# A two-layer graph kernel: left scores routed through memory, weights loaded beside the first rows of x, a third adjacency buffer, degrees taken in layer 1, and the last pair finished tile by tile

## The reference, cut to what matters

```python
deg = jnp.maximum((adj != 0).astype(jnp.float32).sum(-1), 1.0)
h = jnp.maximum(_layernorm(x), 0.0)                  # x: 3327 x 256, adj: 3327 x 3327 of 0 and 1
# layer 0, with adj as both adjacencies
attn_a = sigmoid(concat([adj @ h, h]) @ Wa.T + ba)   # one number per row; attn_b the same with Wb
hs = h @ W_sa
s_left, s_right = hs @ a_sa[0, :256], hs @ a_sa[0, 256:]
e = where(adj != 0, exp(-leaky_relu(s_left[:, None] + s_right[None, :], 0.01)), 0)
x_a = (e / (sum(e, axis=1) + 1e-5)) @ hs
x_b = adj @ (h @ W_gcnb) + b_gcnb
x = x + sigmoid(attn_a * x_a + attn_b * x_b)
# layer 1
h = jnp.maximum(_layernorm(x), 0.0)
pooled = (adj + I) / deg @ h + h                     # deg**-0.5 on both sides, per row
x = x + relu(pooled @ W + b)
```

## Time and profile before

| | |
|---|---|
| median of 3 runs | 653.65 us (652.34 to 656.84) |
| the profiled execution's own time | 648.95 us |
| its span, first to last instruction | 647.1 us |
| PE busy | 617.8 us, 95% of the span |
| PE on the chain that ended last | 87% of the span |
| DVE / ACT / POOL busy | 438.2 / 365.3 / 271.5 us |
| mean granted PE clock | 0.986 of full speed |

### The profile page before, as it was taken

The page is one execution under the profiler, slowest core; times in us unless marked ns, Lnnn a source line. Parts: engine busy times, 40 slices in busy tenths (PEclk is TensorE's granted clock), DMA queues, the critical chain, the costliest instruction groups (busy, mean ns, idle before and its releaser), DMA issues.

```text
span 647.1 us, 13487 instructions
## 1 busy us (share of the span) xinstructions
PE 617.8 (95%) x5333; PEld 528.0 (82%) x5333; DVE 438.2 (68%) x869; ACT 365.3 (56%) x877; POOL 271.5 (42%) x378
## 2 busy tenths in 40 slices
PE   6777999999999999999999999999999799999994
PEld 3445677888888888888888888888888688888883
DVE  4577665799999898989898988988752323122131
ACT  2566676779888787878787777879632000000000
POOL 3547463355435162435353366313134253425331
PEclk9798999999999999999999999999999999999998
DMA  8904572397364554656563644000010365555521
GB/s 201 194 4 131 81 170 44 50 195 180 51 164 89 124 142 74 156 80 160 73 164 53 164 50 58 2 1 2 1 51 2 115 244 172 171 161 178 183 76 32
DMA packets 38549, 68.62 MB, mean 106 GB/s; under 512 B 3159, under 2 KB 30809, under 8 KB 37079
## 3 DMA queue, kind: packets, MB, share of 16 engines
q0 software_dynamic: 28544, 22.15, 23.6%
q1 hardware_dynamic: 7906, 41.68, 19.8%
q10 hardware_dynamic: 2037, 3.94, 2.3%
HBM read 67.74 MB, written 22.15 MB: 139 GB/s over the span
## 4 chain that ended last, share of the span: by engine, by line
PE 87%; POOL 4%; DVE 3%; issue 2%; DMA 1%; ACT 1%; ACTq 0%; POOLq 0%; DVEq 0%
PE accE L703 11%; PE accE L705 11%; PE accA L682 11%; PE accE L704 11%; PE accA L683 11%; PE accA L755 8%; PE accA L754 8%; PE accE L754 4%; PE accE L755 4%; POOL diag L337 1%; PE tp L610 1%; POOL stage L317 1%; PE pw L726 1%; PE pw L727 1%; PE pw L728 1%
## 5 line engine op out<-in xcount | busy, mean ns | idle before, releaser
L703 PE MATMUL accE<-HI,Z 128*128 128x257 f16 x676 | 184.3, 273 | 0.0
L705 PE MATMUL accE<-HI,E 128*128 128x257 f16 x676 | 184.1, 272 | 0.0
L704 PE MATMUL accE<-LO,Z 128*128 128x256 f16 x676 | 183.9, 272 | 0.0
L485 ACT ACTIVATE Z<-LO,sr 128x256 f32<-128x256 f32 x338 | 151.3, 497 | 40.0 <-PE accE L705 40.0
L682 PE MATMUL accA<-HI,adjT 128*128 128x258 f16 x676 | 154.1, 273 | 0.0
L683 PE MATMUL accA<-LO,adjT 128*128 128x258 f16 x676 | 154.0, 273 | 0.0
L494 ACT ACTIVATE Z<-Z,sr 128x256 f32<-128x256 f32 x338 | 150.2, 497 | 0.1
L945 DVE TENSOR_TENSOR E<-Z 128x512 bf16<-128x512 f32 x169 | 140.7, 832 | 5.8
L939 DVE TENSOR_TENSOR Z<-adjT,Z 128x512 f32<-128x512 bf16 x169 | 120.3, 712 | 18.8 <-ACT Z L494 18.6
L755 PE MATMUL accA<-LO,adjT 128*128 128x256 f16 x468 | 103.5, 273 | 0.0
L754 PE MATMUL accA<-HI,adjT 128*128 128x257 f16 x468 | 103.5, 273 | 0.0
(11 more groups left out here) (116 smaller groups left out, 761.6 us busy)
## 6 DMA issues: line engine op xcount, KB each, us to landing
adjT_store<-adjT SPq DMA_DIRECT2D x11, 1664.0 KB, 6.7
adjT<-adjT_store SPq DMA_DIRECT2D x11, 896.0 KB, 4.7
stage<-in_adj_dram POOLq DMA_DIRECT2D x48, 192.0 KB, 5.0
adjT<-adjT_store SPq DMA_DIRECT2D x11, 768.0 KB, 6.3
stage<-in_adj_dram POOLq DMA_DIRECT2D x36, 224.0 KB, 8.1
out_dram<-late ACTq DMA_DIRECT2D x12, 256.0 KB
stage<-in_adj_dram POOLq DMA_DIRECT2D x12, 223.5 KB, 9.7
xs<-in_x_dram SPq DMA_DIRECT2D x5, 256.0 KB, 6.0
```

Source lines behind the costliest of these rows:

```text
L485: ins = act.activation(Z[:, n % RING, v], slw[:, m], ACT.Relu, bias=sr99[:, t:t + 1], scale=1.0 - SLOPE)
L703: pe.matmul(dst[:, 0:D + 1], zhi, HI[:, t, 0:D + 1], start=(t == 0), stop=False)
L704: pe.matmul(dst[:, 0:D], zhi, LO[:, t, 0:D], start=False, stop=False)
L705: ins = pe.matmul(dst[:, 0:D + 1], zlo, HI[:, t, 0:D + 1], start=False, stop=(t == TILES - 1))
```

## The change

Five edits go together.

1. **Left scores through memory.** `diag`, `widen` and `left` go. SP stores the left-score column of a pair to a DRAM tensor `sl_store` (256 elements of 4 bytes), waits for it to land, and reads it back to `slw` with the same 1 KB row for all 128 partitions. `leaky(m, 0)` waits for that.
2. **Start.** The first x rows and the weights share the SP and ACT queues; DVE takes the first row statistics before the weight maxima; `dense(0)` comes ahead of `turn(1)` and `project(0)` on PE; throwaway matmuls are placed anew (44 in place of 50).
3. **Third buffer.** In layer 2 the raw adjacency buffer `stage` serves as a third buffer (`adj1`), used by `k` = 2, 5, 8, 11. The fillers around the last dense steps now take `pooled(2, ...)`.
4. **Degrees from layer 1.** The HI matmul of `neighbours` is 260 columns wide, with the ones column at its head; ACT copies the degree (`degs`); one DVE step inverts them all. `HI1` loses its ones column, and `output` is two fused operations per tile plus one.
5. **Last pair by tile.** For `k` = 12 all matmuls of tile 0 come first, then those of tile 1; output and store follow for each tile.

The diff, cut to its core:

```diff
+        adj1 = [adjT[1][:], adjT[0][:],
+                stage[:].rearrange("p e b q -> p (e b q)").rearrange("p (u e i v) -> p u e i v", u=PAIRS, e=2, v=2)]
...
         def _(sp):
-            for k, w in enumerate((W_sa, W_g)):
-                sp.dma_start(wsg[k], w.rearrange("(h p) o -> p h o", p=P)).then_inc(wsg_in, 16)
-            load_x(sp, 0, (2, 3))
+            load_x(sp, 0, (0, 1))
+            sp.dma_start(wsg[0], W_sa.rearrange("(h p) o -> p h o", p=P)).then_inc(wsg_in, 16)
...
+            def spread_left(i):
+                sp.wait_ge(srw_ok, i + 1)
+                sp.dma_start(bass.AP(sl_store.tensor, 2 * P * i, [[1, P], [P, 2]]), srw[:, 2 * i:2 * i + 2, 3],
+                             allow_slow_non_contiguous=True).then_inc(sl_out, 16)
+                sp.wait_ge(sl_out, 16 * (i + 1))
+                if i >= 1:
+                    sp.wait_ge(sl_in, 16 * i)
+                sp.dma_start(slw[:, i], bass.AP(sl_store.tensor, 2 * P * i, [[0, P], [1, 2 * P]])).then_inc(sl_in, 16)
...
+            for i in range(PAIRS):
+                spread_left(i)
+                if i == 0:
+                    sp.dma_start(w1, W1.rearrange("(h p) o -> p h o", p=P)).then_inc(w1_in, 16)
...
+                if i == 6:
+                    keep_adj(0)
+            for m in range(1, LAST - 1):
+                keep_adj(m)
...
+            sp.wait_ge(tr_ok, NC * PAIRS)
             for k in range(2, PAIRS):
                 for c, (u0, u1) in enumerate(CHUNKS):
-                    sp.wait_ge(part_done[c], k - 1)
-                    dst = adjT[(k + 1) % 2][:, u0:u1].rearrange("p u e i v -> p (u e i v)").bitcast(U32)
+                    if k >= 3:
+                        sp.wait_ge(part_done[c], k - 2)
+                    dst = adj1[k % 3][:, u0:u1].rearrange("p u e i v -> p (u e i v)").bitcast(U32)
...
             def score_parts(i):
...
-                if i >= 1:
-                    pool.wait_ge(wide, i)
-                for e in range(2):
-                    ins = pool.tensor_scalar(diag[:, e], ident[:], srw[:, 2 * i + e, 3:4], None, ALU.mult)
-                ins.then_inc(diag_ok, 1)
...
-            def widen(i):
-                pe.wait_ge(diag_ok, i + 1)
-                pe.matmul(pw[:, 256:512], ones[:], diag[:].rearrange("p e n -> p (e n)"), start=True,
-                          stop=True).then_inc(wide, 1)
...
-                        dst = bank(accA[m % 2], e)[:, 0:D + 2]
-                        pe.matmul(dst, w, HI[:, t, G0:HIW], start=(t == 0), stop=False)
-                        ins = pe.matmul(dst, w, LO[:, t, D:LOW], start=False, stop=(t == TILES - 1))
+                        dst = bank(accA[m % 2], e)
+                        pe.matmul(dst[:, 0:D + 4], w, HI[:, t, ONE:HIW], start=(t == 0), stop=False)
+                        ins = pe.matmul(dst[:, 2:D + 4], w, LO[:, t, D:LOW], start=False, stop=(t == TILES - 1))
...
             for s in range(PAIRS):
                 dense(s)
-                if s < 2:
-                    keep_busy(4)
-                widen(s)
+                if s == 0:
+                    turn(1)
+                    project(0)
...
-            row_stats(0)
-            scales(0, 3, 1)
-            minus_mean(0)
-            row_stats(1)
-            score_weights()
-            minus_mean(1)
+            row_stats(0)
+            gate_weights()
+            dve.wait_ge(wsg_in, 32)
+            largest(0, 2)
+            minus_mean(0)
+            largest(2, 3)
+            on_diagonal(0, 3)
+            row_stats(1)
+            scales(0, 3, 1)
+            turned_second(0)
...
+            for k in range(3, LAST):
                 for u in range(PAIRS):
                     pooled(k, u)
+            for e in range(2):
+                pooled_tile(LAST, e)
```

More of the change, by code:

```diff
@@ L90, in gnn_kernel @@
         wrows = sb("wrows", [8, P])
-        diag = sb("diag", [P, 2, P])
         ones = sb("ones", [P, P])
@@ L218, in gnn_kernel @@
         hi1_ok = sem("hi1_ok")
-        one1_ok = sem("one1_ok")
         lo1_ok = sem("lo1_ok")
-        adj_ld = [[sem(f"adj_ld{c}_{b}") for b in range(2)] for c in range(NC)]
+        adj_ld = [[sem(f"adj_ld{c}_{b}") for b in range(3)] for c in range(NC)]
         part_done = [sem(f"part_done{c}") for c in range(NC)]
@@ L260, in out_count @@
         def out_count(k, b):
-            return 16 * sum(3 if ORDER[j] == LAST else 1 for j in range(k + 1) if j % 2 == b)
+            return 16 * sum({LAST: 3, LAST - 2: 2}.get(ORDER[j], 1) for j in range(k + 1) if j % 2 == b)
         block = ctx.enter_context(nc.Block())
@@ L276, in _, with keep_adj @@
             load_x(sp, 3)
[L277 to L281, removed]
+            def spread_left(i):
[6 more added lines that the diff above has]
+                sp.dma_start(slw[:, i], bass.AP(sl_store.tensor, 2 * P * i, [[0, P], [1, 2 * P]])).then_inc(sl_in, 16)
+            def keep_adj(m):
                 sp.wait_ge(tr_ok, NC * (m + 1))
@@ L469, in first_halves @@
                     act.activation(dst, src[:, e], ACT.Copy).then_inc(hi_ok, 1)
-            def left(i):
-                act.wait_ge(wide, i + 1)
-                act.activation(slw[:, i], pw[:, 256:512], ACT.Copy).then_inc(sl_ok, 1)
             def leaky(m, u):
                 n = m * PAIRS + u
-                if n == 0:
-                    act.wait_ge(sl_ok, 1)
+                if u == 0:
+                    act.wait_ge(sl_in, 16 * (m + 1))
                 if m == 0:
@@ L538, in _ @@
             first_weights(1)
+            norm(1)
             for s in range(PAIRS + 5):
@@ L587, in store_out @@
                 m = ORDER[k]
+                if k == LAST:
+                    for e in range(2):
+                        act.wait_ge(o_ok, k + 1 + e)
+                        dst = bass.AP(out.tensor, (m * 64 + e) * D, [[QN * D, 4], [2 * D, QUAD], [1, D]])
+                        act.dma_start(dst, osb[k % 2][:, e]).then_inc(o_out[k % 2], 16)
+                    return
                 act.wait_ge(o_ok, k + 1)
@@ L1116, in output, with output_tile @@
                     dve.wait_ge(o_out[k % 2], out_count(k - 2, k % 2))
-                dve.scalar_tensor_tensor(out=osb[k % 2], in0=wx[:], scalar=0.0, in1=xs[:, 2 * m:2 * m + 2],
+                dve.scalar_tensor_tensor(out=osb[k % 2], in0=[wx, wm][k % 2][:], scalar=0.0, in1=xs[:, 2 * m:2 * m + 2],
                                          op0=ALU.max, op1=ALU.add).then_inc(o_ok, 1)
-            for k in range(PAIRS):
+            def output_tile(k, e):
+                dve.wait_ge(tile_done, e + 1)
+                dve.wait_ge(hpw_ok, k + 1)
+                dve.wait_ge(o_ok, k - 1)
+                pooled_out(k, e)
+                dve.wait_ge(y_ok, 2 * k + 1 + e)
+                dve.wait_ge(o_out[k % 2], out_count(k - 2, k % 2))
+                dve.scalar_tensor_tensor(out=osb[k % 2][:, e], in0=[wx, wm][k % 2][:, e], scalar=0.0,
+                                         in1=xs[:, 2 * ORDER[k] + e],
+                                         op0=ALU.max, op1=ALU.add).then_inc(o_ok, 1)
+            degrees()
+            for k in range(LAST):
                 output(k)
+            for e in range(2):
+                output_tile(LAST, e)
 _INS = ['x', 'adj', 'L0_gnn_W_sa', 'L0_gnn_a_sa', 'L0_gnn_W_gcnb', 'L0_gnn_b_gcnb', 'L0_gnn_Wa', 'L0_gnn_ba',
```

159 lines of the change are left out of this document (88 added, 71 removed).

## The result

| | before | after |
|---|---|---|
| median of four runs each | 655.25 us | 687.91 us |
| ratio, 95% interval | | 1.0505 [1.0447, 1.0563] |
| span of the profiled execution | 647.1 us | 682.7 us |

The change made the kernel 5% slower; 634.8 us (629 to 642) had been forecast. The two traces differ by 35.6 us, and they split it cleanly. The first transposes of layer 2's dense part started at 158.83 before and at 204.40 now: +45.6 us. From there to the same work of pair 11: 330.9 before, 331.2 now. From there to the first DVE operation behind the last matmul: 148.35 and 142.4, -6.0. From there to the end: 9.0 and 4.7, -4.3. So everything is lost ahead of these transposes, and the gains behind them are there.

What follows compares the result with a forecast made beforehand. PE was taken as busy throughout the long stretches, with gains left in the opening, float32 wide products, a layer 2 hole and the tail. -11 + 0.6 - 0.3 - 5.3 - 2.8 = -18.8 from 653.65 gave 634.8 us, range 629 to 642.

Steps and rivals of the forecast that it cites:

- T: Time of one left-score round trip through memory in SP's queue; 6.5 us would land the second adjacency store at 122.6, in time.
- third rival: SP's queue too slow: second adjacency store waits behind thirteen serial round trips; slower from T = 9.5, 667 us at 10.5; chance 0.06.
- the cover: Opening: new left-score transfers stay hidden, leaving at 20.5 and back by 32, before ACT needs them near 38.6 us; no cost.
- Start: Opening on PE: dense(0) starts at 16.2 us, 3.1 us earlier than before.
- Opening, pair by pair: Up to 60 us: dense products come earlier; -11 us, of which 5.6 is removed matmul time; bounds -13.5 and -6.
- the chain: Opening: each engine's order with old trace durations; dense products gain 3.9 us at the first, 10.2 at the sixth.
- Wider matmuls: Layer 1 neighbour matmuls: 676 HI matmuls grow from 258 to 260 columns, +0.6 us; bounds 0 and +2.
- Third buffer: Layer 2: wait for k = 2's second chunk and half clock after it go, -5.3 us; HI matmuls one column narrower, -0.3.
- Tail: Behind the last matmul: fewer DVE operations, -1.85 us, and a smaller last store, -1.0; -2.8 us in all.
- Rivals one and two: One: DVE holds the opening, which gives 6 us, 639.8, chance 0.19. Two: new wait in layer 2, 640.1, chance 0.08.

Runs made afterwards that it cites:

- (4): Kernel before plus scratch stores of a constant in layer 1, alone in SP's queue; 256 side-by-side 4-byte elements took 12.7, 10.7, 9.1 us issue to issue.
- (8): Kernel with 512-byte score rows, plus 12 throwaway matmuls before pair 1's dense product: 627.89 us; instead third buffer undone: 635.89; instead last pair as a pair: 633.41.
- (7): Changed kernel with each pair's score columns turned into two rows on PE, stored as 2 elements of 512 bytes: 629.06 us, ratio to before 0.9632.
- (2): Changed kernel with the float32 wide product back (diag, widen, left; nothing through memory), other four parts kept: 643.96 us, ratio to before 0.9824.
- 6: Changed kernel with left scores stored as 8-byte elements: 627.83 and 637.58 us; with second adjacency store also moved behind the ninth round trip: 625.73 us.

## Why the prediction was wrong

**The step that failed** is T = 6.5 us in the third rival, the time of a round trip, and in it the landing of the score column, for which the cover had put 5.9 us. Because of it the sum put the new transfers at nothing. Measured: the store landed in 11.8 us in the median of thirteen (7.5 to 14.5), T was 11.9, and the second adjacency store went out at 174.53. The other part of the cover, that the first row is back by 32, was late too (its read-back went out at 31.88 and took 4.7 us), but ACT reached its first score step only at 41.40, so this cost nothing.

The rival had the right place: the second adjacency store behind all round trips. Its form was right only in part, and that its figure agrees with the total is partly luck. By its line PE stands 13 T - 104 us for that store; with the measured 11.9 this is 51, and PE stood 52.3 for DVE in all, but 38.1 for the second store. The store landed at 183.0 and not at 192.8, since the first adjacency store, for which the line adds 8.8, took hardly a turn of its own in the series, and DVE came to the transpose that needs it at 141.8 and not at 125.5. It came late there because it had already waited 4.9 us for an adjacency load and 10.5 us for the first adjacency store, which the prediction did not price; PE's hole of 10.0 us stands behind the second of these.

The landing came from the nearest row of the same element size, the bias load of 5.9 us. That row reads 4-byte elements from memory; the new transfer writes them, side by side, and that took 9.1 to 12.7 us with nothing else in SP's queue (4). The argument against the rival, that the transfer engines are busy only 0.28 of the time, was empty: about half of the landing passed behind the store's last packet (5.5 of 11.8 us in the median), where idle engines are no help. Given that 6.5 left the store in time "by little", and that each microsecond of T costs 13, 0.06 was far too low a chance. The rule below 512 bytes that I cited from the Trainium skill ("DMA: Bandwidth & Descriptors", Specifications) warned of a slow store, and I set it aside with a row that did not measure the same thing. For the landing its limit is not what the runs show: 128 elements of 64 bytes took 4.7 and 4.8 us, 128 of 512 bytes 4.8 and 4.9. No run measured the rate, of which it speaks.

**Start:** forecast `dense(0)` at 16.2; it came at 15.82. Right.

**Opening, pair by pair:** forecast 24.4, 29.3, 34.9, 39.1, 46.1, 53.9; measured 23.9, 30.7, 36.0, 41.9, 48.6, 55.7. The gain at `dense(6)` was 8.4 us where the chain said 10.2; half clock came back at pairs 1 and 3 (granted clock 0.50 from 24 to 27 us and 0.51 from 36 to 39). Taking one such stretch away brought the next dense product 2.1 us forward (8), about as much as the difference. With a store that lands in time (7) the first transposes of layer 2 came at 150.29, 8.5 us earlier than before; with 8-byte elements and the moved store at 145.75, 13.1 earlier. The forecast of 11 lies between: right in size, once the transfers are hidden. The gain needs the wide product to go: with it in place the one trace shows none (2).

**Wider matmuls:** forecast +0.6; a pair took 30.36 us instead of 30.33, +0.3 over eleven pairs. Right in kind, half the size.

**Third buffer:** forecast -5.3 and -0.3; measured -6.0, and +6.8 when undone. Right.

**Tail:** forecast -2.8; measured -4.3. The mechanism was right. DVE's part was (2.8 to 0.94 us, -1.9); the last store's was forecast too small: the 6.2 us from DVE's end to the end of the span became 3.8, -2.4 instead of -1.0.

**Rivals one and two:** neither came. DVE did not hold the opening at 6 us, and no wait stood in layer 2.

So the sum of -18.8 fits what the change would have been without the landing, as far as the kernels of 6 and 7 tell, which differ from it in more than that: they ended at 625.7 and 629.1, by the traces 23.1 and 18.5 us below before, by the medians 28.1 and 23.6.

## What to carry to other kernels

A transfer that is off the path still has a place in its queue: multiply the time of a round trip by the number that stands ahead of the next thing somebody waits for, and compare with the moment when it is wanted; if little is left, measure the one transfer before trusting the sum. Take a landing from a row with the same direction, element size and neighbourhood, not only the same size. To spread a column through memory, bring it into rows or at least into elements of 8 bytes first.

## What the runs showed of the hardware that was not expected

- A store of 64 or more 4-byte elements side by side in device memory lands 5.1 to 8.9 us behind its last packet, in the stretches shown with the transfer engines idle: 6.6 to 12.7 us from issue to the next issue. The same 256 elements 64 or 512 bytes apart land 0.5 us behind it, 16 side by side 0.4 to 0.7, 128 elements of 8 bytes side by side 1.9 to 2.8, rows of 512 bytes 0.4 to 0.5.
- In the kernel these stores also delay other loads. From 60 to 110 us an adjacency packet took 172 ns in the mean and 7.8 us at most, against 90 ns and 0.7 us with rows of 512 bytes, while the stores' own packets filled 0.02 of the engines' time. One adjacency load that DVE waited for stood 17.4 us on the chain.
